# Attention units of a hybrid layer: all six peak rounds of a unit issued two units ahead, one between each two pieces of the running unit's work

## What is computed

```python
q = q * cos + _rotate_half(q) * sin
k = k * cos + _rotate_half(k) * sin
scores = jnp.einsum('bhqd,bhkd->bhqk', q, k) / math.sqrt(hd)
causal = jnp.triu(jnp.ones((S, S), dtype=bool), k=1)
scores = jnp.where(causal[None, None], -jnp.inf, scores)
attn = jax.nn.softmax(scores, axis=-1)
attn_out = jnp.einsum('bhqk,bhkd->bhqd', attn, v)
```

## Time and profile before

| | |
|---|---|
| Median of three runs | 912.74 us (912.5 to 915.92) |
| The profiled execution | 914.78 us, of which the profile's span is 912.9 us |
| Attention units, from the first score piece of unit 0 to the last outputs of unit 15 | 509.0 to 681.1 us of the span |
| Distance of one unit to the next in there | 10.90 us where written out, 10.95 to 11.15 us within the loop |
| TensorE busy in one unit of 10.90 us | 9.97 us |
| VectorE, ScalarE busy in that unit | 7.41, 5.88 us |
| TensorE's granted clock in that unit | 1.00 of full speed |

### The profile page before, as it was taken

One profiled execution on the slowest core, in us unless ns is written; L12 is line 12 of the kernel. 1 busy time (PEld: TensorE's weight loads), 2 busy tenths in 40 slices (PEclk: granted clock), 3 DMA queues, 4 the chain that ended last, 5 costly groups with the idle time before them and its releaser, 6 DMA issues. The chain is left out here.

```text
span 912.9 us, 19361 instructions
## 1 busy us (share of the span) xinstructions
PE 669.8 (73%) x5374; PEld 465.6 (51%) x5375; DVE 527.9 (58%) x1512; ACT 423.8 (46%) x908; POOL 372.8 (41%) x438
## 2 busy tenths in 40 slices
PE   2993888877921999970264899999986940899990
PEld 1330333334721999970132555555554730899990
DVE  6438899981651555557077566666633453455555
ACT  4215677746300555543342355555565410455560
POOL 6101898974375344454332020000005177245451
PEclk9996999997955999995586799999997965899995
DMA  7889999110011222213247211111001011222215
GB/s 229 321 235 249 246 250 250 34 54 16 13 42 51 76 70 67 67 36 96 65 127 198 67 37 36 37 34 34 19 2 69 1 41 52 65 74 67 69 46 147
DMA packets 89440, 84.15 MB, mean 92 GB/s; under 512 B 12448, under 2 KB 79640, under 8 KB 89112
## 3 DMA queue, kind: packets, MB, share of 16 engines
q1 hardware_dynamic: 83736, 71.73, 29.7%
q0 software_dynamic: 5632, 11.58, 3.9%
HBM read 37.95 MB, written 45.33 MB: 91 GB/s over the span
## 5 line engine op out<-in xcount | busy, mean ns | idle before, releaser
L1516 DVE TENSOR_REDUCE t_peak<-bank 128x1 f32<-128x512 f32 (+2 forms) x192 | 107.4, 597 | 50.0 <-PE bank L1632 49.3
L794 POOL TENSOR_TENSOR UN<-m_work 128x512 f32<-128x512 f32 x64 | 80.5, 1268 | 72.6 <-DVE m_work L974 71.8
L415 ACT ACTIVATE m_dx_tiles<-bank,m_e_b1all 128x128 f32<-128x128 f32 x224 | 63.9, 368 | 62.4 <-PE bank L636 60.2
L415 ACT ACTIVATE t_v_tiles<-bank,t_e_b1all 128x128 f32<-128x128 f32 x224 | 63.9, 368 | 62.3 <-PE bank L636 61.6
L380 POOL DMA_INDIRECT results<-m_XC,m_e_to_row x56 | 55.8, 996 | 65.7 <-issue 33.5
L380 POOL DMA_INDIRECT results<-t_A,t_e_to_row x56 | 55.7, 995 | 65.6 <-issue 31.4
L974 DVE TENSOR_TENSOR_SCAN m_work<-bank,m_work 128x512 f32<-128x512 f32 x64 | 76.7, 1215 | 7.3 <-POOL UN L794 5.6
L1097 PE MATMUL bank<-UN,ident 128*128 128x512 f32 x128 | 70.7, 634 | 13.9 <-POOL UN L794 13.0
L525 DVE COPY UN<-w1all 128x512 f32 x112 | 48.0, 429 | 46.2 <-PE bank L636 37.0
L1352 POOL COPY t_tabs<-t_v_tiles 128x128 f32 (+1 forms) x16 | 4.6, 291 | 169.0 <-PE bank L1689 165.7
L636 PE MATMUL bank<-t_A,UN 128*128 128x128 f32 x448 | 61.3, 281 | 0.0
(11 more groups left out here) (332 smaller groups left out, 1550.3 us busy)
## 6 DMA issues: line engine op xcount, KB each, us to landing
xrows<-m_nothing SPq DMA_DIRECT2D x25, 1032.0 KB, 17.5
w1all<-in_e_w SPq DMA_DIRECT2D x6, 1024.0 KB, 12.1
m_dx_tiles<-xrows SPq DMA_DIRECT2D x56, 64.5 KB
t_v_tiles<-xrows SPq DMA_DIRECT2D x56, 64.5 KB
stacks<-t_front SPq DMA_DIRECT2D x24, 128.0 KB, 2.4
stacks<-t_hT SPq DMA_DIRECT2D x24, 128.0 KB, 2.4
t_tabs<-stacks SPq DMA_DIRECT2D x32, 96.0 KB, 2.2
t_hT<-stacks SPq DMA_DIRECT2D x32, 96.0 KB, 2.2
```

Source lines behind the costliest of these rows:

```text
L415: ins = act.activation(e.hid[:, mp, f * P:f * P + P], core.tiles(2 + mp)[:, f, :], ACT.Gelu, bias=row(e.b1all, x)[:, f:f + 1])
L794: g.tensor_tensor(hc[:, k % 4, :], h[:, k % 2, :], c_sb[:, k % 2, :], ALU.mult).then_inc(hc_ready, 1)
L1516: v.tensor_reduce(peak[p][:, qt, a, ss[0]:ss[-1] + 1], bank[:, ACROSS[a], 0:len(ss) * w].rearrange("p (j n) -> p j n", n=w), AX_X, ALU.max ...
```

## The change

It moves work and adds and removes none, save two waits in TensorE's order (`unit_in` is waited for earlier, and `oT_ready`, which `turn_output` waits for, is now also waited for ahead of `outputs` 0, which comes ahead of `turn_output` now).

In the step of unit u TensorE now issues no round of unit u + 1. It issues all six of unit u + 2: score piece 0, round 0, piece 1, last outputs of u - 1, round 1, pieces 2 and 3, round 2, `outputs` 0, round 3, `turn_output` of u - 1, piece 4, round 4, `outputs` 1, `turn_shift` of u + 1, `outputs` 3, round 5. VectorE reads round 0 of u + 2, splits u + 1, reads rounds 1 to 3, normalises u - 1, and reads rounds 4 and 5. `prepare` does all six rounds of unit 1 as well, with `turn_shift` of unit 0 after the first of them. The steps of units 14 and 15 hold no rounds.

```diff
@@ vector: prepare, step
                 split_peaks(0, 0)
-                read_peaks(1, 1, 0)
-                read_peaks(1, 1, 1)
+                for n in range(len(PEAKS)):
+                    read_peaks(1, 1, n)
...
+                if more > 1:
+                    read_peaks(u + 2, p, 0)
                 if more:
-                    for n in range(2, len(PEAKS)):
-                        read_peaks(u + 1, 1 - p, n)
                     split_peaks(u + 1, 1 - p)
+                if more > 1:
+                    for n in range(1, 4):
+                        read_peaks(u + 2, p, n)
                 if not first:
                     normalise(u - 1)
                 if more > 1:
-                    read_peaks(u + 2, p, 0)
-                    read_peaks(u + 2, p, 1)
+                    for n in range(4, len(PEAKS)):
+                        read_peaks(u + 2, p, n)
@@ tensor: prepare
-                turn_shift(0, 0)
                 pe.wait_ge(unit_in[1], 64)
                 peaks(1, 1, 0)
-                peaks(1, 1, 1)
+                turn_shift(0, 0)
+                for n in range(1, len(PEAKS)):
+                    peaks(1, 1, n)
@@ tensor: step
-                next_peaks(2)
                 pe.wait_ge(low_ready, LEAD + u + 1)
                 scores(u, q, 0)
+                if more > 1:
+                    pe.wait_ge(unit_in[q2], 64 * (i2 + 1))
+                coming_peaks(0)
                 scores(u, q, 1)
-                next_peaks(3)
                 if not first:
                     last_outputs(u - 1, 1 - p)
+                coming_peaks(1)
                 scores(u, q, 2)
-                next_peaks(4)
                 scores(u, q, 3)
+                coming_peaks(2)
+                pe.wait_ge(va_ready, LEAD + u + 1)
+                pe.wait_ge(exp_ready, LEAD + STEPS * u + 2)
+                if not first:
+                    pe.wait_ge(oT_ready, LEAD + u)
+                outputs(p, 0).then_inc(av_done[0], 1)
+                coming_peaks(3)
                 if not first:
                     turn_output(u - 1)
-                next_peaks(5)
-                pe.wait_ge(va_ready, LEAD + u + 1)
-                pe.wait_ge(exp_ready, LEAD + STEPS * u + 2)
-                outputs(p, 0).then_inc(av_done[0], 1)
-                if more > 1:
-                    pe.wait_ge(unit_in[q2], 64 * (i2 + 1))
-                later_peaks(0)
                 scores(u, q, 4)
+                coming_peaks(4)
+                pe.wait_ge(exp_ready, LEAD + STEPS * u + 4)
+                outputs(p, 1)
                 if more:
                     turn_shift(u + 1, 1 - p)
-                pe.wait_ge(exp_ready, LEAD + STEPS * u + 4)
-                outputs(p, 1)
                 outputs(p, 3).then_inc(av_done[1], 1)
-                later_peaks(1)
+                coming_peaks(5)
```

More of the change, by code:

```diff
@@ L1703, in step, with coming_peaks @@
             def step(u, i, q, more, first=False):
[L1704 to L1710, removed]
+                p, (i2, q2) = q % 2, after(i, q, 2)
+                def coming_peaks(n):
                     if more > 1:
                         peaks(u + 2, q2, n)
-                next_peaks(2)
                 pe.wait_ge(low_ready, LEAD + u + 1)
                 scores(u, q, 0)
+                if more > 1:
+                    pe.wait_ge(unit_in[q2], 64 * (i2 + 1))
+                coming_peaks(0)
                 scores(u, q, 1)
-                next_peaks(3)
                 if not first:
                     last_outputs(u - 1, 1 - p)
+                coming_peaks(1)
                 scores(u, q, 2)
-                next_peaks(4)
                 scores(u, q, 3)
+                coming_peaks(2)
[5 more added lines that the diff above has]
+                coming_peaks(3)
                 if not first:
                     turn_output(u - 1)
-                next_peaks(5)
-                pe.wait_ge(va_ready, LEAD + u + 1)
-                pe.wait_ge(exp_ready, LEAD + STEPS * u + 2)
-                outputs(p, 0).then_inc(av_done[0], 1)
-                if more > 1:
-                    pe.wait_ge(unit_in[q2], 64 * (i2 + 1))
-                later_peaks(0)
                 scores(u, q, 4)
+                coming_peaks(4)
+                pe.wait_ge(exp_ready, LEAD + STEPS * u + 4)
+                outputs(p, 1)
                 if more:
                     turn_shift(u + 1, 1 - p)
-                pe.wait_ge(exp_ready, LEAD + STEPS * u + 4)
-                outputs(p, 1)
                 outputs(p, 3).then_inc(av_done[1], 1)
-                later_peaks(1)
+                coming_peaks(5)
             sweep(pe, prepare, step)
```

## The result

The changed kernel takes 903.0 us in the median of four runs (902.22 to 903.07), the kernel before 912.95 us (912.5 to 915.92). The ratio is 0.9873, with a 95% interval of 0.9851 to 0.9895, so it is about 1.3% faster. The profiled execution took 903.06 us, its span 901.2 us.

The account below looks back on a forecast made before the run. TensorE was taken to set the unit's time, stalling where rounds 1 and 2 touch until VectorE reads the peaks. + 3.4 - 11.9 - 1.3 = - 9.8 us gave a median of 902.9 us, range of 8 in 10 897.5 to 909.5.

Parts of the forecast that it names:

- The sum: Whole kernel: start + 3.4, 14 units - 11.9, end - 1.3, together - 9.8 us.
- 1.30 - 0.35 - 0.10: Gain a unit, 0.85 us: the most winnable at touching rounds 1 and 2, less late second halves and split outputs.
- The charge for late second halves: Between rounds: half of 0.3 + 0.2 + 0.2 us of missing work, 0.35 us a unit, bounds 0 and 0.7.
- the distance was even: Round 5 to round 0: piece 0 only, 0.55 us, but round 5 itself takes 0.57 us, so nothing short.
- said to be 0.3 us short: Round 0 to round 1: piece 1 and last outputs give 1.12 us of the 1.4 us needed.
- the rivals: Gain partly eaten (0.14), shift's chain (0.1), halves apart everywhere (0.05), change not doing what it says (0.01), no stalls (0.1).
- the rule: Work needed between rounds for VectorE's two reads: about 1.4 us behind 512 columns, 1.2 behind 384, 0.8 behind round 5.
- Splitting the outputs: `outputs` 1 parted from 3 by another kind of matmul: charged 0.1 us a unit, bounds 0 and 0.34.
- the bound by idle time: TensorE's idle time in a unit, 0.93 us, as the least to win; 13.0 us over 14 units.
- the predicted 0.05 us to spare: `low_ready`, from `turn_shift` to piece 0: 1.14 us of TensorE work against 1.09 us for the shift's chain.
- The start and the end: First score piece later by 3.4 us (3.0 to 4.0); unit 14's step shorter by 1.3 us (0.9 to 1.6).
- the 1.5 us for the first round ahead of the turn: In `prepare`, round 0 of unit 1 goes ahead of `turn_shift`, so VectorE's reads start 1.5 us sooner.

Follow-up runs that it names:

- `e1_touch`: Changed kernel with round 2 put back right behind round 1, all rounds still two units ahead; 921.41 us, ratio 1.0069.
- `e2_part`: Kernel before with one edit: round 2 of unit u + 1 moved from ahead of score piece 0 to behind it; 910.76 us, ratio 0.9942.
- `e7_rotated`: Changed kernel's places and widths, but the first four places hold rounds of unit u + 1, as deep as the kernel before; 901.45 us, ratio 0.9842.
- `e9_round5_early`: Changed kernel with round 5 moved from behind `outputs` 3 to ahead of it; 903.55 us, ratio 0.986.
- `e4_shift_early`: Changed kernel with `turn_shift` moved ahead of `outputs` 1, so that `outputs` 1 and 3 stand together; 901.31 us, ratio 0.9852.
- `e5_shift_late`: Changed kernel with `turn_shift` moved behind `outputs` 3; 904.28 us, ratio 0.9868.
- `e6_start`: Changed kernel with the start in the old order, unit 0's `turn_shift` ahead of round 0 of unit 1; 905.54 us, ratio 0.9893.
- the control: The changed kernel itself, unedited, timed again beside the kernel before; 903.89 us, ratio 0.9856.
- `e10_both_early`: Changed kernel with `turn_shift` ahead of `outputs` 1 and round 5 between `outputs` 1 and 3; 904.89 us, ratio 0.9871.

## Why the prediction was right

**The bound and its place.** The stall between rounds 1 and 2 was the cause: putting it back with the depth kept costs 1.35 us a unit (`e1_touch`), softening it with the old depth wins 0.28 (`e2_part`), and removing it at the old depth wins as much as the change does (`e7_rotated`). These three show it. The depth of two units has no worth of its own.

**The size of the gain.** The sum said 14 units at 0.85 us, 11.9 us; it was 13.44 us in the two traces. In the units written out, 0.85 us is right: 10.90 to 10.02 or 10.03 is 0.88. The term that was mis-sized is the number of 14 equal units: I took the unit written out for all. The eight units of the loop took 11.05 us and went to 10.02 as well, 1.04 us each before rounding; the other five written out won 0.88 each; and unit 0, part of which runs at the lower clock, went from 12.35 to 11.62 us, 0.73. Together this is the 13.44. In the loop the stall is no longer than elsewhere: from round 1 to the first score piece it is 1.97 to 2.07 us, as in the units written out. What the loop's units had on top stands ahead of `turn_shift`. Piece 4 and the start of `turn_shift` in a loop unit of the kernel before:

```profile
594.10 0.28 PE L1658 MATMUL bank<-t_hT 48*128 48x256 bf16 x2
...
595.05 0.38 PE L1641 MATMUL bank<-identb,t_shift 128*128 128x128 bf16 x4
```

From the one to the other it is 0.95 us there and 0.78 in the earlier trace rows; over the loop's units it is 0.08 to 0.27 us more than 0.78, 0.17 in the mean. The profile names no engine that TensorE waits for at this place, and in the new order, where `turn_shift` stands behind `outputs` 1, the time is gone. Why it was there stays open.

**What was charged against it.** 1.30 - 0.35 - 0.10. Of the two rounds 1.98 - 0.91 = 1.07 us came back, less than 1.30, since round 2 costs 0.57 us and not 0.34. Other work got cheaper too, round 3 from 0.56 to 0.38, round 5 from 0.57 to 0.40 and piece 4 from 0.78 to 0.68 us, which the sum didn't have. The charge for late second halves, 0.35 us, was paid mostly at one place: pieces 0 and 1 grew by 0.51 us about round 0, where the prediction said the distance was even, while round 1, said to be 0.3 us short, has its halves together (534.50, x2). So 0.85 us is right as a sum, by errors that cancel, and the places are not: that is luck in part. Of the rivals none came, since second halves wait at two of the six places and not at most. The reason for the wrong places is in the rule: it counted a round's own work as 0.57 us for round 5 and 0.34 for others, and the reads of round 5 as 0.7 us, but round 5 takes 0.40 us, and its reads start only when all of it is nearly done (541.61 to 542.16). `e9_round5_early` shows it. Splitting the outputs cost 0.13 us by `e4_shift_early`, 0.10 as charged.

**By the busy time or by the distances.** The Trainium skill's rule against busy time ("Trainium Kernel Development and Optimization", Best Practices) is borne out here: TensorE's busy time in the same unit went from 9.97 to 10.02 us while the unit fell by 0.88, and `e4_shift_early` and `e9_round5_early` took a unit that was busy for all its time down to 9.89 and 9.93 us with the same matmuls. The change's own 0.88 us stay under the bound by idle time, 0.93 us; `e4_shift_early`, 1.01 us under the kernel before, goes beyond it.

**The waits that move.** `oT_ready` and `unit_in` show in no wait of TensorE, as said. `low_ready` seems to have the predicted 0.05 us to spare (541.96, 542.01). But piece 0 starts 0.05 us behind the copy in `e5_shift_late` too, where it does wait for it (547.52, 547.57), so nothing is to spare. That it came out so near is luck: `outputs` 3 takes 0.36 us and not 0.25, and round 5 0.40 and not 0.57. The wait stands beside another, that of round 0's second half for the read of round 5, so neither alone sets the unit. In unit 14's step, where no round stands behind `outputs` 3, it is the bound, 0.33 us.

**The start and the end.** 3.4 us was said, 3.07 to 3.10 it was; the 1.5 us for the first round ahead of the turn are 1.55 in `e6_start`. The end was 1.3, and is 1.09 us. The first score piece was foretold at about 512.3 us and came at 510.34, because the attention began 1.76 us sooner.

**The total.** The traces give + 3.07 - 13.44 - 1.09 = - 11.5 us for the change's own stretches, and the ratio of the runs gives 0.0127 x 912.95 = 11.6 us. In the control's group the medians differ by 11.1 us. The sum said 9.8 us; the difference of the first medians, 9.95 us, lies nearer to it than all of these. That 902.9 and 903.0 us agree to 0.1 us is luck: the change wins some 1.7 us more than the sum had, and medians here settle little below 3 us. In the profiled execution, for one, the turn of `A` cost 1.6 us more at the lower clock than in the control.

## What to carry to other kernels

Where one engine fills a buffer and another must empty it before the next fill, look for fills that touch: the stall isn't a question of either engine's load but of how much other work stands between, and the distance to keep can be read from the trace (here 1.88 us from the start of a 512-column round to the second half of the next). Put the round that is emptied fastest where the shortest stretch of other work follows. And spacing doesn't need depth: the same places can be filled from the coming unit and the one after, with less to do ahead of the first step.

## What the runs showed of the hardware

The time at which TensorE's clock rose in the first unit wandered more than I had thought. By the mean clock of 2 us windows it rose some 3.6 us behind the first score piece in `e2_part`, 5 in the kernel before and in `e6_start`, 5.5 in the control, 6.1 in the profile after, 8.5 in `e7_rotated`, 10.8 in `e5_shift_late`, 11.0 in `e10_both_early` and 12.3 us in `e1_touch`, all with TensorE nearly always busy in between. The changed kernel and its control run the same program and differ by 0.6 us; the other kernels have one trace each, so how much of the spread is theirs and how much is chance isn't known. The window of `e5_shift_late` in which it rose:

```profile
524.00:526.00 2.00, 2.00 (x34) 1.50 (x34) 1.32 (x3) 0.97 (x1) 0.00 (x0) 0.79 0.00 0
```

The first unit took 13.59 us there and 11.34 in the control. At the end of the attention the clock fell to 0.51 in the profile after, behind two short waits of 0.81 and 0.79 us, and the turn of `A` took 3.59 us. In the control the waits are the same, the clock stayed at 1.00, and the turn took 1.97 us. The windows of the profile after:

```profile
668.00:670.00 2.00, 0.63 (x4) 0.42 (x4) 0.54 (x4) 1.79 (x2) 0.00 (x0) 1.00 0.00 0
670.00:672.00 2.00, 1.93 (x9) 1.94 (x10) 0.19 (x4) 0.60 (x1) 0.00 (x0) 0.51 0.00 0
```

With the start of the attention wandering by up to 5.8 us on top of it, single medians of this kernel tell differences under 3 us badly, and distances within a stretch tell them well.
